# A graph and expert network on one core: a new tail that interleaves its stages and sums four rows of queries per product

## What is computed

```python
x = x + gnn0(layernorm(x), adj)              # 4 heads
x = x + product_key_attention(layernorm(x))  # 8 heads, 16 gathered rows per head and token, causal
x = x + gnn1(layernorm(x), adj, H_v)
x = x + experts(layernorm(x), router, W1, b1, W2, b2)

def gnn1(inputs, adj, H_v):
    scores = inputs @ H_v                    # one score per token
    logits = where(adj != 0, adj * scores[None, :], -max)
    e = where(adj != 0, exp(logits - rowmax), 0)
    return (e / sum(e)) @ inputs

def experts(x):                              # 32 experts, hidden width 32 each
    idx = argmax(x @ router_w.T + router_b)  # one expert per token
    h = relu(x @ W1[idx] + b1[idx])
    return relu(h @ W2[idx] + b2[idx])
```

## Time and profile before

| | |
|---|---|
| median of 3 runs | 3210.93 us (3207.45 to 3212.22) |
| profiled execution, own time | 3208.43 us |
| its span, first to last instruction | 3206.6 us |
| PE / PEld busy | 2155.2 / 1480.6 us (67% / 46%) |
| DVE / ACT / POOL busy | 1779.0 / 1039.7 / 1997.1 us (55% / 32% / 62%) |
| mean granted TensorE clock | 0.807 of full speed |

### The profile page before, as it was taken

One profiled execution on the slowest core, in us unless ns is written; L12 is line 12 of the kernel. 1 busy time (PEld: TensorE's weight loads), 2 busy tenths in 40 slices (PEclk: granted clock), 3 DMA queues, 4 the chain that ended last, 5 costly groups with the idle time before them and its releaser, 6 DMA issues.

```text
span 3206.6 us, 42220 instructions
## 1 busy us (share of the span) xinstructions
PE 2155.2 (67%) x14008; PEld 1480.6 (46%) x14066; DVE 1779.0 (55%) x6185; ACT 1039.7 (32%) x1966; POOL 1997.1 (62%) x2078
## 2 busy tenths in 40 slices
PE   5255565657575757576768687777878676846776
PEld 4134333434343535354545455555545354534555
DVE  3637564647474746565656656665646463135453
ACT  3133232323232423242424343333434232323332
POOL 0066777777777777777777777777676767740000
PEclk8667676767687868797978888898989797977888
DMA  2023434343434343434343434444343434331110
GB/s 59 15 84 106 132 111 137 112 138 110 138 113 136 115 135 113 135 114 138 113 136 113 135 111 122 122 120 124 100 122 100 122 103 124 110 117 69 60 60 20
DMA packets 164633, 348.21 MB, mean 109 GB/s; under 512 B 38816, under 2 KB 91712, under 8 KB 160192
## 3 DMA queue, kind: packets, MB, share of 16 engines
q0 software_dynamic: 98624, 269.62, 29.3%
q1 hardware_dynamic: 65792, 75.90, 7.3%
HBM read 333.83 MB, written 11.53 MB: 108 GB/s over the span
## 4 chain that ended last, share of the span: by engine, by line
POOL 35%; PE 24%; DVE 16%; issue 14%; ACT 7%; DVEq 2%; DMA 2%; SPq 0%; ACTq 0%; POOLq 0%
POOL ring L632 35%; PE acc L711 7%; PE turn L702 4%; PE wide L818 3%; DVE kv L1181 2%; DMA ring<-in_kv_table,idxT 2%; PE rowsum L683 1%; ACT pt_sb L916 1%; PE wide L762 1%; ACT att_p L971 1%; DVE att_m L1209 1%; ACT att_p L1020 1%; PE wide L365 1%; PE turn L374 1%; PE wide L761 1%
## 5 line engine op out<-in xcount | busy, mean ns | idle before, releaser
L632 POOL DMA_INDIRECT ring<-in_kv_table,idxT x2048 | 1986.5, 970 | 854.2 <-issue 607.6
L711 PE MATMUL acc<-kv,pt_sb 128*128 128x128 f32 x3968 | 596.4, 303 | 113.7 <-ACT pt_sb L916 113.2
L683 PE MATMUL rowsum<-ring,w_block 128*32 128x256 f32 x4096 | 351.8, 446 | 410.9 <-DMA ring<-in_kv_table,idxT 405.8
L711 PEld LDWEIGHTS acc<-kv,pt_sb 128*128 128x128 f32 x3968 | 539.8, 212 | 161.6 <-ACT pt_sb L916 161.6
L916 ACT ACTIVATE pt_sb<-turn 128x512 f32<-128x512 f32 (+2 forms) x608 | 328.3, 562 | 407.4 <-PE turn L702 406.8
L683 PEld LDWEIGHTS rowsum<-ring,w_block 128*32 128x32 f32 x4096 | 101.7, 117 | 622.4 <-DMA ring<-in_kv_table,idxT 454.6
L818 PE MATMUL wide<-kv,qT 128*128 128x512 f32 (+3 forms) x576 | 274.4, 613 | 113.5 <-DVE gs L1181 85.9
L1209 DVE TENSOR_REDUCE att_m<-wide 128x1 f32<-128x128 f32 (+14 forms) x120 | 147.0, 1225 | 188.0 <-PE wide L818 182.7
L702 PE MATMUL turn<-ident,kv 128*128 128x128 f32 x1280 | 212.9, 307 | 54.6 <-ACT kv L385 24.6
L1181 DVE CUSTOM_DVE_ANT_0 kv<-wide,att_p 128x2048 f32<-128x2048 f32 x56 | 128.3, 2292 | 207.9 <-ACT att_p L971 204.7
L818 PEld LDWEIGHTS wide<-kv,qT 128*128 128x128 f32 x576 | 114.5, 216 | 246.7 <-issue 246.7
(11 more groups left out here) (228 smaller groups left out, 3151.6 us busy)
## 6 DMA issues: line engine op xcount, KB each, us to landing
kv<-in_adj SPq DMA_DIRECT2D x32, 1024.0 KB, 5.1
ring<-in_kv_table,idxT POOLq DMA_INDIRECT x2048
wq_pair<-in_Wq SPq DMA_DIRECT2D x64, 128.0 KB
v_dram<-sums_sb SPq DMA_DIRECT2D x128, 64.0 KB
kv<-v_dram SPq DMA_DIRECT2D x16, 512.0 KB
att_p<-in_Wo SPq DMA_DIRECT2D x16, 512.0 KB, 5.5
xt<-in_x SPq DMA_DIRECT2D x16, 64.0 KB
x_dram<-x SPq DMA_DIRECT2D x16, 64.0 KB
```

Source lines behind the costliest of these rows:

```text
L632: pool.indirect_dma_start(ring[:, slot, i, :], None, kv_table, bass.IndirectOffsetOnAxis(idxT[:, r % 2, u:u + 1], 0))\
L683: mm = pe.matmul(rowsum[32 * k:32 * k + 32, 0:ROW], w_block[:, at:at + 32], ring[:, slot, k, :], start=(tk == 0), stop=(tk == 3))
L711: mm = pe.matmul(dst, pt_sb[:, q % 2, b * P:(b + 1) * P], rhs(4 * q + b), start=(q + b == 0), stop=(q == len(widths) - 1 and b == widths[q ...
```

## The change

The tail of every engine is written anew.

- **Order.** `plan_last` makes one list of stages that all engines follow: L (logits and exponential of row i), T (transposes of row i), A (product of four rows), B (residual, norm and router), C (choice of the expert), H (hidden layer), Y (output layer), Z (last addition and store). The experts of a round stand between the rows of the next.
- **Four rows per product.** The transposed weights of four rows are kept side by side (`weights_T`, 512 columns), and A is 16 products of 512 columns with the stationary operand `xn1T` instead of 64 products of 128 columns. The result is transposed: ACT copies it (`mix_T`) and PE turns it back. The output layer is done likewise, in 9 products of 512 columns.
- **Hidden layer.** The expert choice is added to the product in PSUM as 0 or -1e30, so the relu on ACT masks it; DVE's 8 multiplications per round go.
- **Earlier work.** Tiles 0 to 14 are normalized in the four steps of query tile 15 (`prepare_mix`), and the scores of 12 tiles go out in the last `end` item; in it DVE makes the mask of rows 0 to 3 and their logits over the first 1536 columns (`far_logits`). ACT issues the loads of rows 0 to 4. Six row buffers, in parts of `kv` that are free by then, replace two; a row is now a view of 4 pieces of 512.
- The stores go from POOL to SP.

```diff
+        def plan_last():
+            order = []
+            for i in range(T + 1):
+                u, place = i // 4 - 1, i % 4
+                if i < T:
+                    order.append(("L", i))
+                if u >= 0 and place == 2:
+                    order.append(("B", u))
+                if u >= 0 and place == 3:
+                    order.append(("C", u))
+                if u >= 1 and place == 0 and i < T:
+                    order.append(("H", u - 1))
+                if u >= 1 and place == 1:
+                    order += [("Y", u - 1), ("Z", u - 1)]
+                if i > 0:
+                    order.append(("T", i - 1))
+                if u >= 0 and place == 0:
+                    order.append(("A", u))
+            last = T // 4 - 1
+            return order + [("H", last - 1), ("Y", last - 1), ("B", last), ("Z", last - 1), ("C", last), ("H", last),
+                            ("Y", last), ("Z", last)]
...
+            def sum_rows(u):
+                pe.wait_ge(mix_copied, 4 * CH * (u + 1))
+                for b in range(T):
+                    mm = pe.matmul(acc[:, :], xn1T[:, b, :], weights_T[u % 2][b // 4][:, b % 4, :],
+                                   start=(b == 0), stop=(b == T - 1))
+                mm.then_inc(mix_summed, 1)
+                pe.wait_ge(mix_taken, u + 1)
+                after(pe, x3_made, u)
...
+            def hidden(u):
+                pe.wait_ge(hot_in, u + 1)
+                pe.wait_ge(t_sel, 1)
                 for c in range(EC):
...
+                    after(pe, hid_relu, EC * u + c - 1)
+                    bank = wide[:, (c % 2) * 512:(c % 2 + 1) * 512]
+                    pe.matmul(bank, w1_sb[:, c * P:(c + 1) * P], xn3T.rearrange("p j n -> p (j n)"), start=True, stop=False)
+                    pe.matmul(bank, sel_expert[:, c, :], onehotTb, start=False, stop=True).then_inc(hid_made, 1)
...
+            for stage, i in last_order:
+                if stage == "L":
+                    act.wait_ge(mix_logit, logits_done(i))
+                    act.activation(adj_row[i % 6], adj_row[i % 6], ACT.Exp, bias=mix_nm[:, i:i + 1],
+                                   accum_out=mix_sum[:, i:i + 1]).then_inc(mix_exp, 1)
...
+            first_logits()
+            for stage, i in last_order:
+                if stage == "L" and i >= FIRST:
+                    logits(i)
+                elif stage == "B":
+                    residual(i)
+                elif stage == "C":
+                    expert(i)
+                elif stage == "Z":
+                    dve.wait_ge(moe_back, i + 1)
...
+                if it["last"]:
+                    show_scores(0, T - 4, 1)
...
+            def far_logits():
+
+                take_sums()
+                dve.wait_ge(score_in, 1)
+                for i in range(FIRST):
+                    dve.wait_ge(adj_row_in[i], 16)
+                    dve.tensor_scalar(first_hide[i].rearrange("p (c n) -> p c n", c=CH), adj_row[i], 0.0, HIDE,
+                                      ALU.is_equal, ALU.mult)
```

More of the change, by code:

```diff
@@ L47, in graph @@
         count["heads"] += 4
-        add("end", [0, 0, 0], (1,), g=g, k=None, hide=g + 1)
+        add("end", [0, 0, 0], (1,), g=g, k=None, hide=g + 1, last=False)
     def step(fetch, g=None, k=None, q=None, s=0, end=(0, 0, 0), close=True):
@@ L57, in step @@
             hide = g_end + 1 if g_end is not None and g_end + 1 < tiles else None
-            add("end", end, (1,), g=g_end if close else None, k=k_end, hide=hide)
+            add("end", end, (1,), g=g_end if close else None, k=k_end, hide=hide, last=q == tiles - 1)
         return None if close else g_end
@@ L283, in build_network @@
             sem("mid_" + n) for n in "xt adj hide x1 x1out xn1 xn1T xn1Tin x1back x2 x2out".split()]
-        hv_in, t_w, t_sel, t_x2, t_adj0, t_adj1, t_out = [
-            sem("last_" + n) for n in "hv w sel x2 adj0 adj1 out".split()]
-        score_rows, score_shown, score_in, mix_logit, mix_exp, mix_turned, mix_copied, mix_summed, x3_made = [
-            sem("mix_" + n) for n in "rows shown in logit exp turned copied summed x3".split()]
-        xn3_made, xn3T_made, xn3T_in, route_made, route_hot, hot_turned, hot_in, hid_made, hid_relu, hid_masked, \
-            moe_made, moe_relu, moe_out = [sem("moe_" + n) for n in
-            "xn3 xn3T xn3Tin route hot turned in hid relu masked made relu2 out".split()]
@@ L291, in build_network @@
-        t_adj = [t_adj0, t_adj1]
+        hv_in, t_w, t_sel = [sem("last_" + n) for n in "hv w sel".split()]
+        t_x2 = [sem(f"last_x2_{b}") for b in range(2)]
+        t_out = [sem(f"last_out{b}") for b in range(2)]
+        adj_row_in = [sem(f"last_adj{i}") for i in range(6)]
+        score_rows, score_shown, score_in, mix_logit, mix_exp, mix_turned, mix_copied, mix_summed, mix_taken, \
+            mix_back, x3_made = [sem("mix_" + n) for n in
+            "rows shown in logit exp turned copied summed taken back x3".split()]
@@ L852, in step, with show_scores @@
                     show_head(it["ahead"])
+            def show_scores(lo, hi, count):
+                pe.wait_ge(score_rows, count)
+                for t in range(lo, hi):
+                    mm = pe.matmul(wide[:, t * P:(t + 1) * P], score_part[t // 4][:, t % 4, :], ident[:, :],
+                                   start=True, stop=True)
+                mm.then_inc(score_shown, 1)
             def turn_xn1(g):
@@ L1056, in end @@
                 fetch(it["fetch"][1])
+                if it["last"]:
+                    act.wait_ge(score_shown, 1)
+                    act.activation(score_b[:, 0:1536], wide[:, 0:1536], ACT.Copy).then_inc(score_in, 1)
                 fetch(it["fetch"][2])
```

401 lines of the change are left out of this document (243 added, 158 removed).

## The result

The changed kernel took 3171.16 us (median of 4 runs, 3170.23 to 3173.43) beside 3207.45 to 3212.22 before (three runs; a fourth took 3307.19, 3% more than the others, and is left out). The ratio is 0.9886, 95% interval 0.9868 to 0.9904: faster by 1.1%, against a forecast of 3173. The profiled execution took 3170.45, its span is 3168.7.

What follows compares the result with a forecast made beforehand. POOL's gathers bound the first part, then a chain between engines. 2893.1 + 22.3 + 52.0 + 69.0 + 55.8 + 64.0 + 6.0 = 3162.2 for DVE's end, 38.0 less than before; 3210.9 - 38.0 = 3173 us, range 3155 to 3197.

Steps and rivals of the forecast that it cites:

- own scores masked: End of the first part: DVE masks the last tile's scores after four far rows, at 2866.1 instead of 2855.18.
- fill to A0: From row 0's exponential to A of round 0: five exponentials, 16 copies and waiting for banks, 22.3 us.
- A0 to A1, with its share of half clock: Round 0's chain from its A to the next A: 52.0 us, with half clock 53.5.
- behind it: Store after DVE's last instruction: 6.4 us as before.
- Prices: Full-clock stage costs in a round: A 14.2 us, Y 8.0, a hidden-layer chunk 1.38.
- the surcharges of the bounds: Possible extra costs in the rounds: +17 us for dearer products, +12 for masks on 4 x 512 views.
- The stops: Middle rounds: PE idle 12 us ahead of the router, DVE idle over 30 us ahead of Z.
- Half clock: PE starts at half rate, mainly the first A and last H: 1.5 + 1 + 1 + 2.5 = 6.0 us.
- An H above 12 us: Sign of being wrong: a hidden layer above 12 us, or A at 17 or more, would make it slower.
- cold bursts: Rival: eight A and H each lose 3.8 us starting at half rate, 30 instead of 6; 3197 us; chance 9%.
- DVE's stops vanish: Rival: interleaving hides all but PE's own work, a round is 45.4 us; 84 us less, 3129; chance 8%.
- The tail at half clock: Rival: clock stays at 0.50 through A, Y and H; 3294 us, slower by 83; chance 5%.

Runs made afterwards that it cites:

- b_before_z: The changed kernel with residual and norm (B) of rounds 1 and 2 ahead of Z in every engine's order; 3150.60 us, 0.9808 of before.
- packed: The changed kernel with the same stages reordered, so B and C find no logits ahead of them on DVE; 3140.65 us, 0.9781 of before.
- packed_warm: packed plus early masks and scores, row 4's exponential moved later, and unread transposes partly filling PE's last-round waits; 3126.68 us, 0.9730 of before.
- far_undo: The changed kernel without the far logits: rows 0 to 3 go wholly behind the last tile's scores; 3155.80 us, 0.9844 of before.

## Why the prediction was right, step by step

| step | forecast | after |
|---|---|---|
| own scores masked | 2866.1 | 2868.66 |
| last tile's x done | 2880.1 | 2882.65 |
| row 0's exponential starts | 2893.1 | 2896.08 |
| fill to A0 | 22.3 | 21.0 |
| A0 to A1, with its share of half clock | 53.5 | 57.7 |
| A1 to A2 | 70.0 | 71.0 |
| A2 to A3 | 56.8 | 55.0 |
| A3 to DVE's end | 66.5 | 65.2 |
| behind it | 6.4 | 2.8 |
| span | 3168.6 | 3168.7 |

The span fits to 0.1 us because errors of 3.7 in the stages and 3.6 at the end cancel: that is luck. What fits in earnest is the chain.

- *Own scores.* The mechanism held, 2.6 us late: PE's scores began 1.75 later (2841.65) and took 5.31 instead of 4.9, and the first mask took 1.84 instead of 1.23.
- *Prices.* A of 14.0 (forecast 14.2), a chunk of 1.37 (1.38) and Y of 8.1 (8.0) hold; the surcharges of the bounds did not come. Masks and products on views of 4 x 512 cost as before (1.22, 2.29, 2.29).
- *The stops.* 12.10 and 11.75 us of PE ahead of the router, 37.56 and 36.04 of DVE ahead of the first two Z (13.44 and 24.59 ahead of the last two, where over 30 was named); b_before_z and packed confirm the cause.
- *Half clock, the term that was mis-sized.* It was 6.0. Measured against 14.0 and 11.0: A0 2.3, H of round 0 4.8 (17.7 less 11.0 and its wait of 1.97), of round 1 3.2, of round 3 2.0, together some 12. An H above 12 us had been named as a sign of being wrong, and it came in three of the four rounds (17.7, 16.3 and 13.0). I had seen only the waits ahead of a burst; the two larger losses come from the wait inside H behind ACT's exponential, which the chain had as mere time. The size is this execution's: behind the same wait, H of round 0 lost 1.6 us in b_before_z.
- *Store.* It was taken as before, 6.4; on SP it is 2.8.

Of the rivals, cold bursts would have cost 30 us; A of rounds 1 to 3, H of round 2 and the Y's ran at 1.00. The rule of the Trainium skill that was weighed there (TensorE: Matmul & The Clock Gate, section "HAM oscillation — how this bites in real kernels") lays the fall to a long wait between bursts. packed_warm shows that it needs none: its waits ahead of H were 1.52, 0.69, 1.02 and 1.24 us, and the clock fell; with them filled it stayed at full rate. "DVE's stops vanish" is not what this change did, but what packed did with another order, at 54 us a round rather than 45 (its sum gives 82 us less, as its 3129 says, and not 84). The tail at half clock did not occur.

Where the 33.9 us of tail came from: 7.4 ahead of row 0's exponential (77.9 to 70.5 from the 17th last gather; the early norms and scores, against the 13.5 that the own mask was delayed by), 26.5 in the rounds. Of these, undoing the interleaving takes 7.9 and undoing the wide products 5.8 (about 8 but for the clock in H); the rest (the hidden layer that no longer waits for DVE's choice, the fill) was not tried apart.

## What to carry to other kernels

Work put into an engine's idle time is free only if it ends before the next instruction in that engine's order is ready, and if it does not slow another engine's critical stream, here the gathers' issues; the far logits failed first the one test, then the other. When stages are interleaved, place on each engine what the slowest neighbour waits for ahead of what merely fills, and give PE ready work in its waits: that order gave 29.9 us, the interleaving itself 7.9. A short wait inside a run of matmuls can cost as much or more by the clock behind it (1.6 to 4.8 us here) as by itself (1.97).

## What was not expected of the hardware

- DVE's masks and products of whole rows lengthen the issue of an indirect gather from 0.95 us to between 1.4 and 2.5.
- The clock's fall shows at no fixed place behind a gap, and it lasts differently long: in H of round 0 the first product after the wait took 1.46 us in after, between the 1.13 and 2.08 of the two rates, and 1.13 in far_undo, with 2.08 for those behind it; in round 1 of after it took 2.07 at once. Two products were slow in b_before_z, five in after.
- 64 products of 128 columns take hardly more than 16 of 512: 14.56 against 14.00 us.
